# A blockwise recurrence: who updates q, who copies the masked products, and in which order

## The reference, cut to what matters

```python
def step(S, inp):
    rt, kt, vt, wt = inp
    kv = kt[..., :, None] * vt[..., None, :]
    y = jnp.einsum('bhi,bhij->bhj', rt, S + u[None, :, :, None] * kv)
    S = wt[..., None] * S + kv
    return (S, y)
```

## Time and profile before

| | us |
|---|---|
| median of 3 runs | 3254.19 |
| lowest, highest | 3253.11, 3262.6 |
| the profiled execution | 3255.01 |
| its span, from first to last instruction | 3253.2 |

### The profile page before, as it was taken

The page is one execution under the profiler, slowest core; times in us unless marked ns, Lnnn a source line. Parts: engine busy times, 40 slices in busy tenths (PEclk is TensorE's granted clock), DMA queues, the critical chain, the costliest instruction groups (busy, mean ns, idle before and its releaser), DMA issues.

```text
span 3253.2 us, 46577 instructions
## 1 busy us (share of the span) xinstructions
PE 2884.9 (89%) x16832; PEld 1771.7 (54%) x16832; DVE 2408.4 (74%) x4601; ACT 1314.2 (40%) x2753; POOL 1454.2 (45%) x1643
## 2 busy tenths in 40 slices
PE   4589989999898998989889898898989989899898
PEld 2236664456644576345763557635565355753567
DVE  7576788667786687866878668786687776877666
ACT  1373234632256323653136531374314732247322
POOL 2134562345524465244643446334462345623454
PEclk7799999999999999999989999999999999999999
DMA  7500043000520015000340002400024000240000
GB/s 160 111 2 1 20 71 69 2 10 14 83 53 2 11 30 91 29 2 10 49 99 2 2 20 40 99 2 2 20 40 99 2 1 20 40 86 2 1 1 14
DMA packets 70483, 114.97 MB, mean 35 GB/s; under 512 B 9323, under 2 KB 62603, under 8 KB 64059
## 3 DMA queue, kind: packets, MB, share of 16 engines
q1 hardware_dynamic: 66963, 110.72, 17.1%
q10 hardware_dynamic: 3264, 0.79, 0.1%
HBM read 74.69 MB, written 33.65 MB: 33 GB/s over the span
## 4 chain that ended last, share of the span: by engine, by line
PE 52%; DVE 22%; POOL 13%; issue 6%; ACT 3%; DMA 2%; SPq 1%; DVEq 0%; POOLq 0%; ACTq 0%
PE PB L1510 7%; PE PB L1425 6%; PE PB L1411 6%; PE PB L1441 6%; PE PB L1525 5%; DVE mxp L1094 5%; DVE arena L1280 4%; PE PB L1565 3%; DVE arena L1289 3%; PE PB L1600 3%; POOL rstd L572 2%; PE PB L1590 2%; DVE attn L997 2%; PE PB L1362 2%; POOL arena L704 2%
## 5 line engine op out<-in xcount | busy, mean ns | idle before, releaser
L1094 DVE TENSOR_REDUCE mxp<-PB 128x1 f32<-128x512 f32 (+3 forms) x1216 | 723.8, 652 | 145.5 <-PE PB L1414 79.8
L824 ACT ACTIVATE arena<-PB 128x512 f32<-128x512 f32 (+3 forms) x1536 | 658.6, 511 | 402.2 <-PE PB L1425 353.8
L1411 PE MATMUL PB<-arena 96*128 96x512 bf16 (+3 forms) x1536 | 463.2, 344 | 48.7 <-DMA arena<-parts 31.0
L1425 PE MATMUL PB<-arena 99*128 99x512 bf16 (+3 forms) x1536 | 445.0, 335 | 64.1 <-DMA arena<-augT 39.2
L675 POOL TENSOR_TENSOR hl<-arena,hh 128x512 fp32r<-128x512 f32 x192 | 251.8, 1315 | 293.4 <-ACT hh L851 291.8
L1441 PE MATMUL PB<-arena 128*32 128x512 f32 (+3 forms) x3072 | 326.5, 499 | 8.5 <-POOL arena L651 8.5
L1411 PEld LDWEIGHTS PB<-arena 96*128 96x128 bf16 x1536 | 151.4, 100 | 280.6 <-ACT arena L824 94.8
L695 POOL TENSOR_TENSOR arena<-arena,xT 128x512 f32<-128x512 f32 x160 | 184.3, 1176 | 261.7 <-DVE arena L1222 261.7
L651 POOL TENSOR_SCALAR_AFFINE_SELECT arena<-arena 128x512 f32<-128x512 f32 x256 | 162.7, 638 | 306.8 <-ACT arena L824 279.5
L1425 PEld LDWEIGHTS PB<-arena 99*128 99x128 bf16 x1536 | 139.2, 99 | 284.1 <-DVE mxp L1094 83.5
L1510 PE MATMUL PB<-xh,wgu 128*128 128x512 f32 x768 | 258.2, 418 | 29.5 <-issue 26.2
(11 more groups left out here) (142 smaller groups left out, 5418.6 us busy)
## 6 DMA issues: line engine op xcount, KB each, us to landing
arena<-parts SPq DMA_DIRECT2D x112, 256.0 KB, 9.3
parts<-arena SPq DMA_DIRECT2D x192, 128.0 KB
arena<-parts SPq DMA_DIRECT2D x16, 768.0 KB, 17.1
arena<-in_x SPq DMA_DIRECT2D x16, 512.0 KB, 7.2
arena<-parts SPq DMA_DIRECT2D x16, 512.0 KB, 19.4
xres<-in_x SPq DMA_DIRECT2D x16, 512.0 KB, 4.5
out<-xres SPq DMA_DIRECT2D x16, 512.0 KB, 13.3
wgu<-arena SPq DMA_DIRECT2D x2, 768.0 KB, 25.5
```

The lines of the kernel that those rows point to most:

```text
L824: act.activation(pt[:, U % 3, h, 0:n], bank(b, "score", t)[:, 0:n], ACT.Exp, scale=DH ** -0.5).then_inc(act_emptied, 1)
L1094: dve.reduce_max(mxp[:, k // 2 % 2, hs[0]:hs[-1] + 1, col:col + 1], bank(b, "max", t)[:, 0:n * len(hs)].rearrange("p (h n) -> p h n", n=n) ...
L1411: last = mm(ps, qst[0:AUG, i // 4, HG * (k // 2) + h, 128 * (i % 4):128 * (i % 4) + 128], kst[0:AUG, s0 // HALF, HG * (k // 2) + h, 0:n], ...
L1425: mm(ps[:, 0:n], kst[0:AUG + 3, j // 4, h, 128 * (j % 4):128 * (j % 4) + 128], qst[0:AUG + 3, f, h, HALF - n:HALF], start=True, stop=True) ...
```

## The change

MASKED becomes 4, so the four banks of level 4 (blocks of 16 rows) are emptied by ScalarE as rectangles, four a bank, 16 partitions x 128 elements each, and no longer by four masked copies of VectorE. From level 4 on, VectorE does the fourth q update (c=1, h=1) too, on 64 partitions, and GpSimd leaves it out. In all levels VectorE first does the q updates of both halves and only then the masked copies of both. `Q_BEFORE[l]` counts VectorE's q updates ahead of level l: three a level up to level 3, four from level 4 on; the semaphore values follow from it. In level 4 VectorE's fourth update waits for GpSimd's last one.

```diff
-MASKED = 5
+MASKED = 4
+Q_BEFORE = [3 * l + max(0, l - MASKED) for l in range(LEVELS + 1)]
...
-                        qv = qd[:, 1, 1, :].rearrange("p (n s m) -> p n s m", s=2, m=m)[:, :, 1, :]
-                        w = tm[:, 1, :].rearrange("p (n s) -> p n s", s=2)[:, :, 0:1].broadcast_to([128, 512 // m, m])
-                        if l:
-                            pool.wait_ge(q3_updated, LEVELS * b + l)
-                        pool.tensor_tensor(qv, qv, w, ALU.mult).then_inc(q3_updated, 1)
+                        if l < MASKED:
+                            qv = qd[:, 1, 1, :].rearrange("p (n s m) -> p n s m", s=2, m=m)[:, :, 1, :]
+                            w = tm[:, 1, :].rearrange("p (n s) -> p n s", s=2)[:, :, 0:1].broadcast_to([128, 512 // m, m])
+                            if l:
+                                pool.wait_ge(q3_updated, MASKED * b + l)
+                            pool.tensor_tensor(qv, qv, w, ALU.mult).then_inc(q3_updated, 1)
...
                         for c in range(NC):
                             wait_filled(dve, b, "level", 4 * l + 2 * c + 1)
-                            for h in (0, 1) if c == 0 else (0,):
+                            for h in (0, 1) if c == 0 or l >= MASKED else (0,):
...
-                                if l:
-                                    dve.wait_ge(q_updated, 3 * LEVELS * b + 3 * (l - 1) + 2 * c + h + 1)
+                                if c and h and l == MASKED:
+                                    dve.wait_ge(q3_updated, MASKED * (b + 1))
+                                elif l:
+                                    dve.wait_ge(q_updated, Q_BEFORE[LEVELS] * b + Q_BEFORE[l - 1] + 2 * c + h + 1)
                                 dve.tensor_tensor(qv, qv, w, ALU.mult).then_inc(q_updated, 1)
+                        for c in range(NC):
                             for q in (0, 1) if l < MASKED else ():
...
-                                    pe.wait_ge(q_updated, 3 * LEVELS * b + 3 * (l - 1) + 2 + c)
-                                    if c:
-                                        pe.wait_ge(q3_updated, LEVELS * b + l)
+                                    pe.wait_ge(q_updated, Q_BEFORE[LEVELS] * b + (Q_BEFORE[l] if c else Q_BEFORE[l - 1] + 2))
+                                    if c and l <= MASKED:
+                                        pe.wait_ge(q3_updated, MASKED * b + l)
```

More of the change, by code:

```diff
@@ L1721, in _ @@
                     wait_emptied(pe, b, "level", LEVELS * 4 - 1)
-                    pe.wait_ge(q_updated, 3 * LEVELS * (b + 1))
-                    pe.wait_ge(q3_updated, LEVELS * (b + 1))
+                    pe.wait_ge(q_updated, Q_BEFORE[LEVELS] * (b + 1))
                     for n in range(4):
```

## The result

| | before | after |
|---|---|---|
| median, us | 3254.19 | 3280.15 |
| lowest, highest of 5 runs | 3250.15, 3262.6 | 3278.69, 3283.43 |
| the profiled execution | 3255.01 | 3283.43 |
| its span | 3253.2 | 3281.7 |

The change makes the kernel slower: after over before is 1.0077 [1.0066, 1.0089], +26.0 us in the medians and +28.4 between the two profiled executions. The forecast was 3277, range 3261 to 3290. Code moved by a few lines: L1284 is now VectorE's q update (before L1280), L1294 its masked copies (L1289), L719 and L725 GpSimd's k and q3 updates (L718, L723), L1700 the level products (L1695), L1711 the transposes (L1706), L1736 the first product of y (L1732), L971 ScalarE's rectangles (L969).

A forecast was written before the change was run, and what follows sets the result against it. VectorE's queue was taken to set the pace, its q updates waiting on GpSimd's. +3.4 (levels 0 to 3) and -0.6 (levels 4 to 6) make +2.8 a batch; 3255.0 + 22.4 = 3277 us, range 3261 to 3290.

The forecast's parts named there:

- Meetings: VectorE and GpSimd two-input updates wait for each other, costing VectorE up to a GpSimd update, 1.10 to 1.50, less overlap.
- the literal reading: VectorE's blocked update needs its whole 0.68 after GpSimd's release, not 0.55: 4 us more over eight batches, giving 3281.
- Levels 0 to 3, +3.4 a batch: Three VectorE updates in a row wait for GpSimd: new losses 5.1 less 1.7 replaced, level 4 opening at 1192.2, not 1188.75.
- The step for level 1: Last bank fills while q01 runs, GpSimd's k1 takes its turn behind it, q10 ends at 1175.9: 1.0 lost.
- Levels 4 to 6, -0.6: Four copies leave VectorE, three q updates come; level 4's opening to end of level 6's k1: 11.9 to 12.0 against 12.57.
- Rectangles costed at nothing: ScalarE's 16 rectangles at level 4, about 0.27 each by the slope, covered by ScalarE's idle time, so no cost.
- The sum: +3.4 in levels 0 to 3 and -0.6 in levels 4 to 6: +2.8 a batch, +22.4 over eight batches.
- The clock rival: Idle stretches before TensorE's second bank bring 1.2 GHz: about 1 a batch on top, 3285; chance 0.12.
- a sign of being wrong: A TensorE clock of 0.5 over several levels was listed among observations that would show the forecast wrong.
- The faster rival: Levels 1 to 3: second half fills after q01, q10 starts first, k1 and q3 run under copies; -1.8 a batch, 3241; chance 0.06.
- the other sign of being wrong: VectorE q updates of 0.68 in levels 1 to 3 were listed as showing the forecast wrong.

The follow-up runs named there:

- e3: Changed kernel with GpSimd's k and q3 updates cut to the first pair of blocks, all waits kept; 3199.46 us, 0.9825 of the kernel before.
- e4: Kernel before with GpSimd's k and q3 updates cut to the first pair of blocks, all waits kept; 3202.1 us, 0.9832.
- e6: Kernel before with MASKED = 4 alone, so ScalarE empties level 4 and GpSimd keeps its q3 update; 3253.55 us, 0.9998.
- e2: Kernel before with the new order alone, all q updates ahead of all masked copies in levels 0 to 4; 3282.75 us, 1.0078.
- e10: Changed kernel run once more, unedited, to look at the time outside the stages; 3281.57 us, 1.008 of the kernel before.
- e5: Changed kernel with VectorE's copies put between its q updates in levels 0 to 3; 3225.76 us, 0.9908 of the kernel before.
- e8: Changed kernel with the old VectorE order, but level 0 alternating copy and q update; 3230.47 us, 0.9919 of the kernel before.
- e1: Changed kernel without its new order: copies of a half directly behind that half's updates, as before; 3251.63 us, 0.9987 of the kernel before.

## Why the prediction was right, point by point

- **The mechanism.** Meetings of two-input updates of VectorE and GpSimd: shown, since without them (e3 against e4) the loss of levels 0 to 3 falls from 3.8 to 0.2 a stage. The Trainium skill (SBUF — State Buffer, section "SBUF: two separate sides") says that of GpSimd and a VectorE instruction with two SBUF inputs one holds the shared ports and the other fully blocks. These runs agree in kind. Taken literally, the rule would make VectorE's updates end 0.68 after GpSimd's, and after showed 0.55 and 0.54. That the literal reading gave 3281, nearer to 3280.15 than 3277, says nothing for it: what is missing to 3280.15 lies outside the stages.
- **Levels 0 to 3, +3.4 a batch.** Measured +3.8 (29.90 against 26.10) in batch 2, and 3.6 in batch 3. In batch 2 the losses are where the steps put them: three updates of 1.9 at level 0, the third of level 1 at 1.67, two of 1.52 and 1.53 at level 2 (3.83 in all), two meetings at level 3 (3.51). Levels 0 and 2 are so in all eight batches. The step for level 1 holds in batch 2 alone: in the other seven VectorE waited for TensorE's fill instead (0.81 in batch 3). In batches 0, 1 and 7 level 3 has one meeting of 1.47 and two short waits for TensorE (0.16 and 0.58 in batch 0). That these waits cost about as much as the meetings they replaced was not foreseen, and the sum holds there by luck. Of the 0.4 missing in batch 2, 0.2 is k0 of level 1, which meets q00 (0.90 instead of 0.71) and was not foreseen; the rest is spread over copies and gaps.
- **Levels 4 to 6, -0.6.** From level 4's opening to the end of k1 of level 6: 1213.63 + 1.05 - 1202.75 = 11.93, against 12.57, so -0.64. That k1 takes 1.05 and no longer 1.55, and the transposes wait 0.32 for it, not 0.81.
- **Rectangles costed at nothing.** 268 ns, against 0.27 by the slope, and TensorE in level 5 on is released by L1284, never by them; e6 has them alone, 0.9998 [0.9989, 1.0007].
- **The sum.** +3.1 a batch in the six batches that had 43.8 before, about +2.1 in the two that had 44.7, +22.5 for 22.4. That the sum agrees to 0.1 is partly luck: the step of batches 6 and 7 (a meeting that before had already) and the 0.2 to 0.4 too little in levels 0 to 3 cancel. The sum left out what lies outside the stages; the remainder between 3277 and 3280.15 is there, +6.0 in the profile.
- **The clock rival.** Its stretches came, its price did not. The windows of the two batches (busy us and count of PE, PEld, DVE, ACT, POOL; granted clock; DMA):

```profile
1179.30:1182.70 3.40, 2.79 (x13) 2.82 (x14) 3.40 (x4) 0.00 (x0) 0.67 (x1) 0.50 0.00 0
1578.70:1585.50 6.80, 5.83 (x26) 5.77 (x27) 5.96 (x7) 0.00 (x0) 1.58 (x2) 0.50 0.00 0
```

  Around and behind the idle stretch of 2.03 the clock is at 1.2 GHz for 3.4 us in batch 2 and for 6.8 us in batch 3. The trace's clock records put 61.4 us at 1.2 GHz into the eight stages, against 20.5 before. Yet the stage is 46.9 in batch 2 (3.4 us at 1.2 GHz), 46.7 in batch 3 (6.8) and 46.9 in batch 1 (10.2, at levels 1 and 3). So a clock of 0.5 at more than one level, named as a sign of being wrong, did appear, without its price.
- **The faster rival.** Its order of events did occur, at level 1 of every batch but batch 2 and at level 3 of batches 0, 1 and 7, and paid almost nothing. The updates of 0.68 in levels 1 to 3, the other sign of being wrong, are these. VectorE in batch 3:

```profile
1582.75 1.61 DVE L1284 TENSOR_TENSOR arena<-arena 64x512 f32<-64x512 f32 x2
1585.17 0.68 DVE L1284 TENSOR_TENSOR arena<-arena 64x512 f32<-64x512 f32 x1 [0.81 <-PE PB L1700]
```

  With TensorE at 1.2 GHz the fill came after q01, so q10 had its 0.68; but VectorE stood idle for 0.81 before it, and the third update ended 3.10 after the first began where batch 2 has 3.32. A meeting was exchanged for a wait 0.2 shorter. In level 2 no batch had it.

What stays open is the time outside the stages: 3.5 us (26.0 between the medians less the stages' 22.5) to 6.0 (between the profiles), in both profiles of the changed kernel and not in e2's. Where it is largest there is also more time at 1.2 GHz, at another place in each profile (e10); its cause isn't shown.

## What to carry to other kernels

Where two engines share something that copies from PSUM don't use, write the queue so that the copies lie opposite the other engine's work; don't set all two-input updates in a row behind the event that also releases the other engine's. The number of operations on each engine says little about it: the changed kernel and e5 have the same operations on every engine, and differ by 54 us (ratios 1.0077 and 0.9908).

To size such a share, shrink the other engine's operations and keep everything else: here that showed 54 us in the kernel before (3256.39 to 3202.1, same chip) and at once that the order by itself costs little. Read it as an upper bound: it also takes away the other engine's own time where something waits for it. Of the 6.0 us a stage, 4.0 lie in levels 0 to 3 (26.10 to 22.11), where VectorE never pauses and only its meetings can have gone; the 2.0 in levels 4 to 6 hold both.

## What the runs showed that I had not expected

- How much the sharing costs the kernel before: its stage falls from 43.8 to 37.8 when GpSimd's updates are small, 6 us of each stage. The prediction took the 1.9 of level 0 as given; e8, with level 0 alone in another order, has 0.72, 0.69 and 0.76 there.
- TensorE's slow stretches often cost a stage nothing here, and sometimes saved it time. In the kernel before, the stages with 3.4 us at 1.2 GHz (batches 0 to 5) took 43.8 and those at 2.4 GHz throughout (6 and 7) took 44.7: the later fill missed a meeting of 1.0. e1 has the same, 42.5 with such a stretch and 43.5 without. It is no rule, though. In e5 the one stage with 3.4 us at 1.2 GHz (batch 0) took 41.7, and the seven without it 40.5. The stretch fell on TensorE's second half of level 2, first batch 0, then batch 2:

```profile
384.50 3.24 PE L1713 MATMUL PB<-arena 128*128 128x128 f32 x16 [1.83 <-DVE arena L1297]
1171.17 2.05 PE L1713 MATMUL PB<-arena 128*128 128x128 f32 x16 [1.83 <-DVE arena L1297]
```

  VectorE then stood idle for 0.60 ahead of level 3, where it had no pause in batch 2.
- VectorE and GpSimd take turns: at level 0 of after, GpSimd's q3 (from 1176.05) waits for VectorE's update that ends at 1176.64, and then ends first, at 1178.02, although VectorE's next is in place at 1176.67.
